# Routing in four batches of four groups instead of five batches of 3, 4, 3, 3 and 3

## What is computed

```python
x = x + _L0_conv_ref(_ln_c(x), ...)          # attention, residual
t = _to_tokens(x)                            # rows of 128 numbers
# inside _L0_ffn_ref, on the normalised tokens:
gate_logits = xf @ Wg + bg
top_w, top_i = jax.lax.top_k(gate_logits, 2)
top_w = jax.nn.softmax(top_w, axis=-1)
for e in range(E):                           # E = 8, D = 128, H = 512
    h = jax.nn.gelu(xf @ W1[e] + b1[e], approximate=False)
    out = out + w_dense[:, e:e + 1] * (h @ W2[e] + b2[e])
x = t + out
```

## Time and profile before

| what | us |
|---|---|
| median of three timed runs (911.72 to 914.72) | 913.08 |
| profiled execution, device time | 913.78 |
| its span | 912.0 |
| busy: PE / DVE / ACT / POOL | 621.5 / 693.4 / 583.5 / 416.9 |
| mean granted TensorE clock, share of full speed | 0.871 |

### The profile page before, as it was taken

One profiled execution on the slowest core, in us unless ns is written; L12 is line 12 of the kernel. 1 busy time (PEld: TensorE's weight loads), 2 busy tenths in 40 slices (PEclk: granted clock), 3 DMA queues, 4 the chain that ended last, 5 costly groups with the idle time before them and its releaser, 6 DMA issues. The chain is left out here.

```text
span 912.0 us, 21482 instructions
## 1 busy us (share of the span) xinstructions
PE 621.5 (68%) x6804; PEld 509.6 (56%) x6804; DVE 693.4 (76%) x2423; ACT 583.5 (64%) x1517; POOL 416.9 (46%) x556
## 2 busy tenths in 40 slices
PE   0006699999998889888888510048999999999100
PEld 0001388877777677776776410047888888888100
DVE  3699579999988998998898369038888888888153
ACT  0015489998998899788878451047788778778100
POOL 3000112221156423545645548717777777777400
PEclk9999689997999899889988555579999999999755
DMA  9933691000000000000000002122322322322499
GB/s 198 222 81 68 193 91 3 3 2 1 2 23 28 26 1 11 26 26 25 31 23 31 28 30 84 45 60 67 84 81 77 83 77 83 81 80 68 92 203 282
DMA packets 61683, 62.01 MB, mean 68 GB/s; under 512 B 20708, under 2 KB 51493, under 8 KB 59912
## 3 DMA queue, kind: packets, MB, share of 16 engines
q1 hardware_dynamic: 51592, 34.28, 18.4%
q0 software_dynamic: 8704, 17.98, 5.9%
q10 hardware_dynamic: 1280, 8.39, 4.2%
HBM read 36.18 MB, written 25.26 MB: 67 GB/s over the span
## 5 line engine op out<-in xcount | busy, mean ns | idle before, releaser
L773 ACT ACTIVATE L<-L,lmin 128x128 f32<-128x128 f32 x512 | 159.6, 398 | 0.2
L700 POOL DMA_INDIRECT expert_out<-yo,rows_all x142 | 140.4, 989 | 41.6 <-issue 21.9
L652 POOL DMA_INDIRECT routed<-pay,pos x128 | 135.6, 1060 | 42.7 <-issue 25.7
L978 DVE CUSTOM_DVE_ANT_0 L<-S,biasN,logit_scale 128x128 f32<-128x128 f32 x512 | 146.1, 346 | 6.3 <-issue 5.8
L631 POOL TENSOR_TENSOR og<-on,rden 128x256 f32<-128x256 f32 x64 | 39.6, 619 | 193.3 <-DVE on L990 191.1
L1225 DVE SCALAR_TENSOR_TENSOR hl<-hf,hscale,hh 128x512 f16<-128x512 f32 x142 | 106.7, 751 | 5.1
L864 ACT ACTIVATE hf<-S,b_sb,inv_hscale 128x256 f32<-128x256 f32 x214 | 105.0, 566 | 2.5 <-PE S L1425 1.5
L620 POOL TENSOR_TENSOR xs<-x,xs 64x512 fp32r<-64x512 f32 x32 | 40.6, 1270 | 126.8 <-ACT xs L749 106.4
L1223 DVE TENSOR_SCALAR hh<-hf,hscale 128x512 f16<-128x512 f32 x142 | 69.6, 490 | 36.7 <-ACT hf L864 29.7
L963 DVE TENSOR_TENSOR pl<-PT,ph 128x512 f16<-128x512 f32 x128 | 84.9, 685 | 13.2 <-ACT ph L768 12.5
L1440 PE MATMUL PT<-w_h,hh 128*128 x568 | 77.8, 218 | 21.5 <-DVE hl L1225 21.5
(11 more groups left out here) (232 smaller groups left out, 1828.1 us busy)
## 6 DMA issues: line engine op xcount, KB each, us to landing
rows_all<-routed SPq DMA_DIRECT2D x71, 132.0 KB
xt<-in_x SPq DMA_DIRECT2D x8, 512.0 KB, 25.6
shared<-in_L_conv_ln_w ACTq DMA_DIRECT2D x8, 512.0 KB, 12.3
shared<-in_L_conv_ln_b ACTq DMA_DIRECT2D x8, 512.0 KB, 10.5
shared<-expert_out SPq DMA_DIRECT2D x16, 256.0 KB, 11.8
pay<-expert_out SPq DMA_DIRECT2D x16, 256.0 KB, 11.3
out<-xt SPq DMA_DIRECT2D x16, 256.0 KB, 9.2
expert_out<-yo,rows_all POOLq DMA_INDIRECT x142
```

Of the source, the lines that this page charges most:

```text
L652: pool.indirect_dma_start(routed, bass.IndirectOffsetOnAxis(ap=pos[:, slot, i:i + 1], axis=0), pay[:, i, :], None).then_inc(scattered[slot ...
L700: pool.indirect_dma_start(expert_out, bass.IndirectOffsetOnAxis(ap=row_place[t % IN_BUFS][:, k, W + 1:W + 2], axis=0), yo[t % YO_BUFS][:, ...
L773: last = nc.scalar.activation(L[p][:, h, i, :], L[p][:, h, i, :], ACT.Exp, scale=-1.0, bias=lmin[p][:, h * R + i:h * R + i + 1])
L978: last = nc.vector.tensor_tensor_reduce(out=L[p][:, h, i, :], in0=S[(4 * u + h) % 3][:, i * P:(i + 1) * P], in1=biasN[:, h, :], scale=logi ...
```

## The change

One line: the sixteen groups are divided into four batches of four instead of five. MOST, the largest number of rows in a batch, is 16 before and after. The carry constants for the scan are made once for each size of batch: two sizes before, one after.

```diff
@@ -95,7 +95,7 @@
     IN_BUFS = 8
     YO_BUFS = 4
     GROUPS = HALF // R
-    PHASES = ((0, 3), (3, 7), (7, 10), (10, 13), (13, 16))
+    PHASES = ((0, 4), (4, 8), (8, 12), (12, 16))
     MOST = R * max(stop - first for first, stop in PHASES)
```

## The result

The kernel after took 905.2 us (median of 7 runs, 903.28 to 907.45), the kernel before 911.72 (7 runs, 909.27 to 914.72): a ratio of 0.993, 95% interval 0.9909 to 0.995. The profiled execution after took 905.2 us; its span is 903.5.

The account below looks back on a forecast made before the run. VectorE's pace bounds attention; afterwards GpSimd's remaining scatters hold back the expert stage. The terms -6.7 - 2.3 + 0.7 + 7.6 = -0.7 us, taken from the median 913.08, gave 912.4 us, range 908.3 to 916.8.

Parts of the forecast that it names:

- Part 3: Up to the last batch's totals: VectorE's chain grows from 3 to 4 groups, 0.7 us lost; GpSimd's 1.3 us covered.
- Part 4: Scatters behind the totals: 39 instead of 33, the 6 more at 1.27 us each, 7.6 us lost.
- Rival C: Scatter tail: each of the 6 added scatters costs the mean interval of 1.64 us; sum +1.5, 914.6 us; chance 0.08.
- Part 1: VectorE's routing work in attention: one batch less gains 6.7 us, bounds 3.7 and 8.8.
- the fourth batch's 7.2 us: Cost read for the old fourth batch, partly in attention's dry steps: 66.5 - 53.1 - 6.2 us.
- Rival B: Attention: the batch that goes was cheap, gain only 4.2 us against 8.3 lost; +4.1, 917.2 us; chance 0.16.
- The price of 9.9 us: Attention: each of three new four-group batches costs as much as the old first batch, 29.7 us together; with growth 10.9 each.
- the 0.26 us a scatter: Attention: what each scatter adds, read from steps 13 to 15, 3.1 us for 12 scatters.
- Part 2: Scatters in attention: 71 issued instead of 80, the 9 fewer gain 2.3 us, between 0 and 2.5.
- Parts 1 and 2: Attention as a whole, batches and scatters together: 9.0 us gained, between 3.7 and 11.3.
- Part 5: The rest, preamble, expert stage and final addition: same expert tiles and instructions, taken as zero.
- Rival A: Attention: VectorE's batch work counts in full, gain 10.2 us; -4.2, 908.9; sign: last residual over 12 us earlier; chance 0.19.

Follow-up runs that it names:

- f3: Kernel before (five batches) with no scatter issued while attention runs, 0 per step instead of 5: 1024.08 us, residuals 365.2 us.
- f4: Kernel after (four batches) with no scatter issued while attention runs, 0 per step instead of 5: 1014.94 us, residuals 356.5 us.
- g2: Kernel after with its last batch split, batches of 4, 4, 4, 2 and 2 groups: 914.7 us, ratio to before 1.0044.
- f1: Kernel before, unchanged, profiled again for the spread of its stages: 910.2 us, residuals 378.5 us.
- f: Group of runs on one chip: both kernels unchanged, and both without scatters in attention; kernel before there 914.62 us (one run).
- j: Group of runs on one chip, the same as f's: four and five batches, both with early issue of free scatters; kernel before there 914.69 us.
- g: Group of runs on one chip: kernel after unchanged, with the last batch split, and with earlier scatter issue; kernel before there 910.79 us.
- g1: Kernel after, unchanged, timed as base for the runs beside it: 905.85 us, ratio to before 0.9945.
- i1: Kernel after, unchanged, timed on a chip where the kernel before took 885.30 us: 886.06 us, ratio 1.0015.
- g3: Kernel after, with every free scatter (7 more) issued at step 36 ahead of the last batch's totals: 899.24 us, ratio to before 0.9884.
- h3: Kernel before, with every free scatter (9 more) issued at step 36 ahead of the last totals: 881.73 us, ratio to before 0.9931.
- j2: Kernel before (five batches) with the early issue of free scatters, on another chip than h3: 906.84 us, ratio to before 0.9918.
- f2: Kernel after, unchanged, profiled again: 910.14 us, residuals 370.3 us, expert tiles 239.2 us.

## Why the prediction was wrong

**Which parts held.** That the change is a trade between attention and the tail, and that the last batch keeps its place. Part 3: +0.7 us up to the totals was forecast, +0.6 came. The 1.3 us by which GpSimd starts later were hidden, as said; its wait ahead of the totals grew to 8.46 us, the earlier one for the last logits went. Part 4: 6 scatters for 7.6 us; the stretch from totals to last scatter grew by 7.61, 60.15 where 60.1 had been forecast. Rival C would have made it 62.3. The blocked issues came twice, 5.18 and 4.09 us. The Trainium skill, "SBUF — State Buffer", section "Who interferes with whom", says that of VectorE and GpSimd the one that issues first has the shared port pair for its whole instruction, while the other blocks. It says so of VectorE's 2-port modes; of an instruction with two SBUF inputs, as w_l's is, it says that it contends with a GpSimd instruction that reads SBUF. The trace agrees with the blocking: the two issues end 0.83 us behind the VectorE instructions beside them, and the four shorter ones 0.84. No run here takes those instructions away.

**Part 1, mis-sized.** This is the step that failed. The gain by one batch less was put at 6.7 us and is 8.8 without scatters (f3, f4). The term with the plainest error is the fourth batch's 7.2 us. It took a step of full attention as the base (53.1 us for five steps) also where attention runs dry, and the bare steps there make 50.6; in f3 the batch cost 9.8, and 7.3 by the old base. Rival B rested on the same 7.2. It had attention gain 4.2 us, and g2 speaks against that, with 7.1 us for a batch of only two groups; whether three groups cost 7.2 or 9.8 there g2 cannot tell. The price of 9.9 us for each of the three new batches was too low as well, even for its bound of 10.9: the first one costs 64.3 - 53.1 = 11.2 us in the profile after, and in f4 they cost 12.5, 12.5 and 9.9. But batches of three groups are dearer there too (11.8 and 10.7), so most of this leaves the difference as it is. In these two runs one batch less gives about the full price of a batch.

The right base alone does not mend the term in the runs with scatters. In f1 the fourth batch's stretch is 64.0 us; less 50.6 and the 6.2 for its scatters it is 7.2 again. Against f3's 60.4 the scatters cost 3.6 there, not 6.2: the 0.26 us a scatter, taken from full steps, does not hold in the dry ones either.

**Part 2, not settled.** The scatters in attention cost 382.1 - 365.2 = 16.9 or 378.5 - 365.2 = 13.3 us before, and 369.0 - 356.5 = 12.5 or 370.3 - 356.5 = 13.8 after. A gain of 2.3 us was forecast. The four pairings give from 4.4 gained to 0.5 lost (16.9 - 12.5 and 13.3 - 13.8), so the runs neither confirm nor refute it.

**Parts 1 and 2 together.** On the chips where before takes 911 to 915 us, the residuals span 382.1, 378.5 and 381.1 us with the five batches of before, and 369.0, 370.3, 368.8, 368.9 and 366.8 with four: on average 11.8 less, where 9.0 was forecast with a bound of 11.3. Up to the residual of step 32 it is 12.3 less, and the two intervals behind it are 0.5 longer. Where it takes 885 to 887 it is 374.4, 374.4, 370.9 and 370.9 against 364.2, 366.4, 368.7 and 365.7: 6.4 less (7.5 less, and 1.1 more). So on the second kind parts 1 and 2 stay below the forecast. Why the gain differs is open.

**Part 5, zero, was no zero.** The expert tiles take 236 to 239.5 us in both kernels on the first kind of chip, and 217 to 231 on the second. A term that I had set aside because its instructions are the same varies by more than the whole forecast. Whether the change moves it isn't shown: it was 2.6 us less after in the first two profiles, 1.8 more in f and 1.1 less in j, and in f and g it follows the group (237.5 to 239.2, and 235.9 to 236.3) more than the kernel. With the terms as measured the first kind of chip gives -11.8 + 8.2 = -3.6 us without the experts, where -4.9 (g1) and -6.5 (the first result) were measured; the remaining 1 to 3 us are no larger than this spread. The second kind gives -6.4 + 8.2 = +1.8, and in i1 the medians differ by +0.8 us (ratio 1.0015, an interval that holds 1). So the 6.5 us of the result are not what the change is worth everywhere.

**The base.** The profiled execution of before, 913.8 us, and the median of three, 913.08, both lay above the median of the seven, 911.72. That accounts for 1.4 us of where the time after was put, not for the size of the change. In the profile of before 3.6 us of attention go with TensorE's clock in the last two intervals. The longer of them lies in the stretch from which part 1 read its 7.2 us and made that reading 2.4 us too high, which hid most of what the base took off it.

**Rival A** had the right direction, and its mark (the last residual over 12 us earlier) was met with 13.6. Its mechanism isn't shown: it asked for 10.2 us from VectorE's work alone, and the pair without scatters gives 8.8, with the prices of single batches between 9.8 and 12.5 where it had 12.2 and 13.2.

## What to carry to other kernels

The price of a piece of work must be read against the same stage without it, not against a full step elsewhere: where a pipeline drains, both the stage and its bare base are shorter. If two terms nearly cancel, the spread of the stages that are "unchanged" decides the sign, so look at more than one execution of them before calling the rest zero. When a queue of issues sets a tail, count what stands behind the last wait, and see whether what is already free can go ahead of it: here this one line gave 6.6 us on the kernel after (g3) and 5.4 and 7.9 on the kernel before (h3, j2), where the change gave 6.5 us less in the result and 0.8 more in i1.

## What the runs showed of the hardware

- The same kernel took 885 and 887 us on two occasions and 911 to 915 on four others. Most of it is in the expert loop, 3.1 against 3.4 us a tile, with the same instructions.
- One loop can hold a rhythm of three unequal tiles (2.7, 3.5, 3.9 us) for 61 tiles and leave it without any change of the program.
- With TensorE's granted clock at 0.58 instead of 0.82, one step of the drained pipeline is 2.4 us longer (12.1 and 9.7), and the next one, at 0.68 and 0.96, 1.2 us. That the clock is the cause isn't shown: f2 took 9.6 us at 1.00 for the former and 7.4 at 0.57 for the latter.
- An indirect DMA of 128 rows costs GpSimd 1.27 us to issue. Issued beside VectorE's long w_l instructions (4.49 us each) it takes 5.0 to 5.2 us beside the first and 4.1 beside the second, in every kernel that was profiled; beside a VectorE subtraction of 1.22 us it takes 1.65 to 1.67. Each of these issues ends 0.8 to 0.9 us behind the VectorE instruction beside it.
